# Spacing the expert and key/value matmuls between the key tiles of a four-layer attention kernel

## Chip, cores and metric

The kernel runs on one NeuronCore of one Trainium2 chip. The metric is the device time of one execution in microseconds (us), given as the median of repeated runs.

## What is computed

Four layers run one after the other on 1024 tokens of width 128. Each is a cross attention with 16 heads of width 8 over 6404 context rows, followed by a mixture of 8 experts. In the third layer (layer 2) the attention weights are a sigmoid, in the others a softmax. Cut to what matters:

```
for l in 0..3:
    h = layernorm(x);  q = h @ Wq.T + bq;  k = ctx @ Wk.T + bk;  v = ctx @ Wv.T + bv
    s = q_h @ k_h.T / sqrt(8)                    # 16 heads, 1024 x 6404 each
    a = sigmoid(s) if l == 2 else softmax(s)
    x = x + concat_h(a_h @ v_h) @ Wo.T + bo
    z = layernorm(x);  w = top-2 routing weights of 8 experts
    x = x + sum_e w_e * expert_e(z)              # gated (silu) in layers 0, 1, 3; gelu in layer 2
                                                 # layer 1 does this twice, on a normalised state
```

The result is x after the fourth layer, 1024 x 128.

## The kernel before, in words

**Tiling.** The 1024 tokens are two blocks of 512 (`QB`). A **unit** u is layer u // 2 and block u % 2 (`unit`), so there are eight. A unit's attention takes four **phases**, one for each group of four heads, so there are 32 phases, 0 to 31. A phase walks over the 6404 keys in 51 **key tiles** of 128. For a key tile the program issues: two `score` steps (each two matmuls, L798, into a pair of PSUM banks), two `exp` steps (ScalarE, L967, one for each pair, 128x1024), and one `av` step for the tile before (four fp32 matmuls, L808, two records of the profile each). In this document a key tile is counted from its first `exp`; a phase begins with every 102nd execution of L967.

**Maxima.** A softmax phase needs each query's largest score beforehand. It is found during the phase before: 176 `max` matmuls (L829, 128 queries by 512 keys, into one of three PSUM banks called `side`), each read by one `red` step of VectorE (L1081, for 32 of them L1085), and 16 `dif` pairs (L820), which ScalarE turns into `above` (`relu`, L975). That makes three to four `max` in each key tile and a `dif` in about every third. In the phases 15 to 22 and in phase 31 there are (almost) none, since the next phase is of the sigmoid layer or does not exist. At the end of a phase (from key tile 48 on) the `max` steps of the phase after the next one begin; they need `fill` (GpSimd, L1295), the copy of that phase's queries.

**Everything else runs beside the attention.** `finish_steps(u - 1)` is what follows the attention of unit u - 1: output projection, layernorm, routing, the experts (`pass_steps`) and the next layer's queries (`qproj`). It is placed into the phases of unit u. `kv_steps(l + 1)` computes keys and values of the next layer, in 13 chunks of two TensorE steps, during the first block of layer l. An expert has six TensorE steps in the gated layers: four `up` (fp32 matmul 128x512, L906) and two `down` (L924); in layer 2 it has eight, four of each. ScalarE reads each `up` with `tanh` and `ac` (L1008, L1017) or with `gc` (L1026), in layer 2 with `upc` (L1032); GpSimd then multiplies (`gatea`, `gateb`, `gatec`: L1362, L1368, L1372, L1378; in layer 2 `hscale`, L1384). In units 3, 4 and 7 VectorE does a part of that.

**PSUM.** The banks are two pairs (`scores`), three single banks (`side`) and one for `av`. `up`, `kv` and `qproj` steps in most units take a *pair* in turn with `score` and `dif`, and use one bank of it (`in_pairs`); `down` takes a `side` bank, in turn with `max`, and keeps it from its first matmul until ScalarE (`yc`) or VectorE has read the sum (`last_use`):

```
    def in_pairs(what, key):
        if what == "up":
            return not by_dve(*key[:2])
        return what in ("score", "dif") or what == "kv" and key[0] < 3 or ...
```

**What sets the order.** No scheduler runs on the chip. `attention_steps` writes one list of steps; each engine executes its own steps in that order, and waits in front of a step for what the step needs. Time in this list is counted in quarters of a key tile (`Q = 4 * KT`). `placed` gives each step of `finish_steps` or `kv_steps` a slot: it adds the gaps that the lists hold, and moves each TensorE step to the next free slot at `at % 4 == 1`. There is one such slot in each key tile, so at most one of these TensorE steps stands in a key tile. With the small gaps of `pass_steps` (0 or 1 inside the experts) that means one in *every* key tile from the first expert to the last. The steps of the other engines and the DMA issues take the slot of the TensorE step that they follow.

Of the kernel before, what the change touches and what calls it, by code (L numbers as in the profile page):

```python
# [118 lines left out]
def softmax(l):  # L119
    return l != 2  # L120


def unit(u):

    return u // 2, u % 2


def phase(p):

    return p // 8, p // NG % 2, p % NG  # L130
# [125 lines left out]
def kv_steps(l):  # L256

    out = []
    for c in range(NCH):
        out.append((1, Step("SP", "ctx", (l, c))))  # L260
        out.append((8, Step("PE", "kv", (l, c, 0))))
        out.append((0, Step("ACT", "kc", (l, c))))
        new = [n for n, (i, pair) in enumerate(SPLITS) if (2 * i + 1 if pair else i) == c]
        out += [(0, Step("POOL", "ksplit", (l, n))) for n in new]
        out.append((8, Step("PE", "kv", (l, c, 1))))
        out.append((0, Step("ACT", "vc", (l, c))))
        out += [(2, Step("SP", "kput", (l, n))) for n in new]
    return out


def norm_steps(u, tag):
    out = []
    if tag in ("f", "a"):
        out += [(2, Step("DVE", "sum", (u, tag))), (1, Step("DVE", "mean", (u, tag))), (1, Step("POOL", "center", (u, tag)))]
    out += [(1, Step("POOL", "square", (u, tag))), (7, Step("DVE", "sumsq", (u, tag))), (1, Step("POOL", "var", (u, tag))),
            (0, Step("POOL", "rstd", (u, tag))), (0, Step("POOL", "scale", (u, tag)))]
    if tag[0] == "r":
        out += [(1, Step("POOL", "weight", (u, tag)))]
    return out


def flip_steps(u, tag):
    return [(8, Step("PE", "xT", (u, tag))), (1, Step("ACT", "xTc", (u, tag)))]
# [82 lines left out]
def finish_steps(u):  # L366

    l, b = unit(u)
    out = []
    if u >= 0:  # L370
        if softmax(l):
            out += [(0, Step("POOL", "bvadd", (u,))), (0, Step("POOL", "boadd", (u,)))]
        out += [(8, Step("PE", "oflip", (u,))), (1, Step("ACT", "oflipc", (u,))), (4, Step("PE", "oproj", (u,))),
                (3, Step("DVE", "resid", (u,)))]
        out += norm_steps(u, "f")
        if l == 1:
            out.append((0, Step("POOL", "zcopy", (u,))))
        for lp in range(FFN[l]["loops"]):
            if l == 1:
                out += norm_steps(u, f"r{lp}")  # L380
            out += flip_steps(u, f"r{lp}" if l == 1 else "f")
            out += pass_steps(u, lp)
        if l == 1:
            out.append((1, Step("POOL", "zadd", (u,))))
    if l < 3:
        out += norm_steps(u, "a") + flip_steps(u, "a")
        for g in range(NG):
            out += [(1, Step("PE", "qproj", (u, g))), (0, Step("ACT", "qsplit", (u, g))), (0, Step("POOL", "qadd", (u, g)))]
    else:
        out.append((2, Step("SP", "out", (b,))))  # L390
    return out


def placed(at, steps, taken):


    out = []
    for gap, s in steps:
        at += gap
        if s is not None and s.eng == "PE":  # L400
            at += (1 - at) % 4
            while at in taken:
                at += 4
            taken.add(at)
        if s is not None:
            out.append((at, s))
    return out


def loads(u):  # L410

    l, b = unit(u)
    out = []
    if b:
        if l + 2 < 4:
            out += [(2, Step("SP", "wattn", (l + 2,))), (0, Step("DVE", "bqs", (l + 2,)))]
        if l + 1 < 4:
            out.append((0, Step("SP", "wo", (l + 1,))))
        out.append((0, Step("SP", "wffn", (l,))))
        if l == 3:  # L420
            out.append((0, Step("DVE", "b1s", (l,))))
    return out
# [3 lines left out]
            routee=1.0, routef=0.5, routeg=0.5, routeh=0.5, routej=0.5, routek=0.5, routel=0.5, routec=1.0, routed=0.4, gatea=0.7, gateb=0.7,  # L426
            ysum=0.7, upc=0.7)
Q = 4 * KT

LEAD = 12  # L430


def attention_steps(units):

    first, last = NG * units[0], NG * units[-1] + NG - 1
    back = []
    taken = set()
    for p in range(first, last + 1):
        at = p * Q
        if p + 1 < 32 and softmax(phase(p + 1)[0]):  # L440
            back += [(at + Q - LEAD - 1, Step("DVE", "fina", (p + 1,))), (at + Q - LEAD - 1, Step("DVE", "finb", (p + 1,))),
                     (at + Q - 7, Step("PE", "flipmax", (p + 1,))), (at + Q - 5, Step("DVE", "finc", (p + 1,)))]
            taken.add(at + Q - 7)
        if p > first:
# [5 lines left out]
        if p + 2 < 32:  # L450
            back.append((at + Q - LEAD - 4 if softmax(phase(p + 2)[0]) else at + 2 * Q - 8, Step("POOL", "fill", (p + 2,))))
            back += [(at + 4 * e + 2, Step("SP", "kload", (p + 2, i))) for i, (a, e) in enumerate(K_PIECES)]
            back += [(at + 6, Step("SP", "kload", (p + 2, len(K_PIECES) + i))) for i in range(NDIF)]
    for u in units:
        at = NG * u * Q
        if u:
            back += placed(at + 16, finish_steps(u - 1), taken)
    for u in units:
        l, b = unit(u)
        at = NG * u * Q  # L460
        back += placed(at + 2, loads(u), taken)
        if b == 0 and l < 3:
            back += placed(at + 24, kv_steps(l + 1), taken)
    back.sort(key=lambda x: x[0])

    def window(p):
# [151 lines left out]
def build(nc, A, out):  # L618
    ctx = ExitStack()
    with ctx:  # L620
# [1143 lines left out]
        with nc.If(n == P):  # L1764
            run(attention_steps(range(8)) + plain(finish_steps(7)))
        with nc.Else():
            layer0 = attention_steps([0, 1])
            masked_unit(0)
            run([s for s in layer0 if s.what not in in_attention + ("kv", "kc", "vc", "ksplit", "kput", "ctx")])
            masked_unit(1)  # L1770
            clear_values(1, 1)
            run([s for s in layer0 if s.what in ("kv", "kc", "vc", "ksplit", "kput", "ctx") or s.what in in_attention
                 and s.key[0] >= 8 and s.what not in ("score", "exp", "av")])
            run(attention_steps(range(2, 8)) + plain(finish_steps(7)))
# [74 lines left out]
```

## Time and profile before

| | |
|---|---|
| runs of the kernel | 4628.06, 4631.72, 4643.15 us; median 4631.72 us |
| the profiled execution, its own time | 4658.06 us |
| its span, first to last instruction | 4656.4 us |
| TensorE busy | 3974.0 us (85%) |
| ScalarE busy | 3939.7 us (85%) |
| VectorE busy | 2807.4 us (60%) |
| GpSimd busy | 830.0 us (18%) |
| granted TensorE clock, mean | 0.959 |

The profile is of one execution. Its span is the time between its first and last instruction; 1.7 us of its own time lie outside. "Busy" is the time in which at least one instruction of the engine runs. The 32 phases fill the span from 195.6 to 4564.7 us; before them lie the opening (first keys and values, first maxima), behind them the experts of unit 7.

### The profile page before, as it was taken

Reading aid. Unit: us, or ns where it says so; the run is one execution under the profiler, and the core shown is the slowest. Engines: PE = TensorE matmul, PEld = TensorE weight load, DVE = VectorE, ACT = ScalarE, POOL = GpSimd, SP = SyncE. Lnnn points to the kernel's source line nnn. Section 1 sums busy time; section 2 is a strip of 40 time slices with the busy share of each in tenths; the row PEclk is TensorE's granted clock in tenths of the full one; section 3 lists DMA queues with packets and bytes.
Section 4 is the critical chain, followed back from the end, with each engine's and each line's share of the span. In section 5 each row is a group of like instructions: output and inputs, shape, how many; then the busy total and the mean of one; then the engine's idle time right before and its main releaser. Section 6 shows DMA issues by size and latency. Waiting matters only on the chain.

```text
span 4656.4 us, 69652 instructions
## 1 busy us (share of the span) xinstructions
PE 3974.0 (85%) x26742; PEld 904.9 (19%) x26742; DVE 2807.4 (60%) x5641; ACT 3939.7 (85%) x4355; POOL 830.0 (18%) x719
## 2 busy tenths in 40 slices
PE   5988888888889888888989999888888888889886
PEld 2121111111122211122212222111111111112112
DVE  2878888778886788867501110110486668877823
ACT  3488998899988898888898889978998889888994
POOL 4010000520034200343412111111000210034002
PEclk8599999999999999999999999999999989999998
DMA  4221001100021110111102121110001100010001
GB/s 125 64 61 35 13 13 29 32 17 14 12 56 36 44 25 18 32 33 35 33 18 73 43 64 31 37 38 16 14 14 36 36 10 12 14 38 27 7 1 49
DMA packets 124485, 151.34 MB, mean 33 GB/s; under 512 B 29272, under 2 KB 76384, under 8 KB 124080
## 3 DMA queue, kind: packets, MB, share of 16 engines
q1 hardware_dynamic: 122640, 145.53, 11.7%
q8 instruction: 212, 3.47, 0.3%
q10 hardware_dynamic: 1504, 1.28, 0.2%
q14 instruction: 129, 1.06, 0.1%
HBM read 123.21 MB, written 23.51 MB: 32 GB/s over the span
## 4 chain that ended last, share of the span: by engine, by line
PE 50%; ACT 23%; DVE 15%; issue 6%; DMA 1%; POOL 0%; SPq 0%; ACTq 0%; POOLq 0%; DVEq 0%
PE av L808 19%; ACT prob L967 14%; DVE mpart L1081 10%; PE scores L798 10%; PE side L829 6%; ACT above L975 6%; PE scores L906 4%; DVE above L1085 4%; PE side L924 4%; PE side L906 2%; ACT ag L1017 1%; PE scores L820 1%; ACT tx L1008 1%; PE scores L948 1%; PE scores L944 1%
## 5 line engine op out<-in xcount | busy, mean ns | idle before, releaser
L967 ACT ACTIVATE prob<-scores 128x1024 f32<-128x1024 f32 x3264 | 3177.9, 1025 | 308.7 <-PE scores L798 293.7
L1081 DVE TENSOR_REDUCE mpart<-side 128x1 f32<-128x512 f32 (+1 forms) x3456 | 2124.3, 656 | 728.9 <-PE side L829 718.0
L808 PE MATMUL av<-prob,VA 128*9 128x512 f32 x6528 | 882.0, 613 | 0.8
L808 PE MATMUL av<-prob,VB 128*9 128x512 f32 x6528 | 867.4, 604 | 1.3 <-ACT prob L967 0.5
L798 PE MATMUL scores<-QP,KA 32*128 32x512 f16 x3264 | 640.1, 394 | 191.7 <-ACT above L975 120.4
L798 PE MATMUL scores<-QP,KB 32*128 32x512 f16 x3264 | 631.6, 389 | 191.4 <-ACT above L975 93.8
L829 PE MATMUL side<-KA,QP 32*128 32x512 f16 (+1 forms) x2112 | 624.7, 392 | 41.5 <-DVE mpart L1081 21.5
L829 PE MATMUL side<-KB,QP 32*128 32x512 f16 (+1 forms) x2112 | 583.0, 383 | 44.6 <-DVE mpart L1081 30.3
L1085 DVE CUSTOM_DVE_ANT_0 above<-side,above 128x512 f32<-128x512 f32 x768 | 513.8, 685 | 76.0 <-PE side L829 69.0
L975 ACT ACTIVATE above<-scores 128x1024 f32<-128x1024 f32 x384 | 393.5, 1025 | 180.9 <-PE scores L820 120.0
L798 PEld LDWEIGHTS scores<-QP,KB 32*128 32x128 f16 x3264 | 151.7, 91 | 865.9 <-ACT prob L967 535.3
L798 PEld LDWEIGHTS scores<-QP,KA 32*128 32x128 f16 x3264 | 151.4, 91 | 820.1 <-ACT prob L967 443.5
L829 PEld LDWEIGHTS side<-KA,QP 32*128 32x128 f16 x2112 | 147.4, 91 | 602.4 <-DVE mpart L1081 450.7
L829 PEld LDWEIGHTS side<-KB,QP 32*128 32x128 f16 x2112 | 140.5, 91 | 590.4 <-DVE mpart L1081 447.3
L906 PE MATMUL scores<-xnT,Fin 128*128 128x512 f32 (+1 forms) x256 | 147.0, 657 | 44.7 <-ACT above L975 31.0
L924 PE MATMUL side<-hT,Fout 128*128 128x512 f32 (+1 forms) x304 | 172.4, 654 | 8.5 <-POOL hT L1384 4.2
L1301 POOL TENSOR_TENSOR o_tok<-o_tok,bvo 128x512 f32<-128x512 f32 x6 | 7.7, 1278 | 898.9 <-DVE o_tok L1122 898.9
L1362 POOL TENSOR_TENSOR ag<-ag 128x512 f32<-128x512 f32 (+1 forms) x80 | 101.6, 1270 | 325.9 <-ACT ag L1026 325.9
L808 PEld LDWEIGHTS av<-prob,VA 128*9 128x9 f32 x6528 | 97.1, 88 | 196.0 <-issue 190.2
L808 PEld LDWEIGHTS av<-prob,VB 128*9 128x9 f32 x6528 | 97.0, 88 | 190.9 <-issue 183.3
L1112 DVE RECIPROCAL rden<-side 128x16 f32<-128x16 f32 x24 | 6.0, 249 | 206.1 <-PE side L847 206.1
L1411 POOL CAST hi<-kb 128x512 f16<-128x512 f32 (+1 forms) x60 | 35.7, 596 | 524.8 <-ACT kb L1056 513.7
(185 smaller groups left out, 2528.9 us busy)
## 6 DMA issues: line engine op xcount, KB each, us to landing
cwb<-weights SPq DMA_DIRECT2D x80, 256.0 KB, 3.9
KA<-kstacks SPq DMA_DIRECT2D x384, 48.0 KB
KB<-kstacks SPq DMA_DIRECT2D x384, 48.0 KB
Fin<-in_Fin SPq DMA_DIRECT2D x64, 256.0 KB, 2.8
kstacks<-hi SPq DMA_DIRECT2D x112, 128.0 KB, 2.4
ctxc<-in_ctxT SPq DMA_DIRECT2D x36, 256.0 KB, 3.0
kstacks<-lo SPq DMA_DIRECT2D x56, 128.0 KB, 2.6
hT<-in_mask SPq DMA_DIRECT2D x16, 400.2 KB, 3.3
```

The lines of the kernel that those rows point to most:

```text
L798: last = pe.matmul(pair[:, j, :], K[p % 2][rows(h), kt * P:kt * P + P], QP[p % 3][rows(h), :], start=True, stop=True)
L808: last = pe.matmul(AV[ROWS * h:ROWS * h + VC, :], V[l % 2][:, kt, g * HG + h, :], prob[:, (e + h // 2) % RING, (h % 2) * QB:(h % 2) * QB + ...
L820: last = pe.matmul(pair[:, j, :], QP[p % 3][rows(h), qt * P:(qt + 1) * P], K[p % 2][rows(h), difference(i)], start=True, stop=True)
L829: pe.matmul(bank[:, 0:chunk_of(c)], QP[p % 3][rows(h), qt * P:(qt + 1) * P], K[p % 2][rows(h), chunk(c)], start=True, stop=True).then_inc( ...
L906: pe.matmul(bank[0:fs, :], Fin[:, w, j * fs:(j + 1) * fs], x[:], start=True, stop=True).then_inc(sem["bgP"], 1)
L924: pe.matmul(bank, Fout[0:fs, w, c, :], h, start=first, stop=c == nk - 1).then_inc(sem["bgP"], 1)
L944: last = pe.matmul(bank[:, 0:w], Wk[l % 2][:], context(l, c)[:, 0:w], start=True, stop=True)
L967: act.activation(prob[:, e % RING, :], pair.rearrange("p a b -> p (a b)"), ACT.Exp if softmax(l) else ACT.Sigmoid, scale=SCALE).then_inc(s ...
L975: act.activation(above[:].rearrange("p a b -> p (a b)"), pair.rearrange("p a b -> p (a b)"), ACT.Relu).then_inc(sem["bgA"], 1)
L1081: dve.tensor_reduce(part, bank, AX.X, ALU.max).then_inc(sem["red"], 1)
L1085: dve.tensor_tensor_reduce(more, bank, more, 1.0, LEAST, ALU.add, ALU.max, part).then_inc(sem["red"], 1)
L1362: pool.tensor_tensor(a, a, g, ALU.mult).then_inc(sem["bgG"], 1)
```

## The change

`placed` gets a parameter `pace`, counted in key tiles. A TensorE step is not placed earlier than `pace` key tiles after the place that the step before it was due (`beat`). With 1.0, the value before, nothing changes. The experts behind the units 0, 1, 2, 5 and 6 get 2.0, 1.7, 1.3, 1.7 and 2.8; the keys and values of layers 1 and 2 get 4.0 and 5.0. Those behind the units 3 and 4 and the keys and values of layer 3, which run where there are no maxima, stay as they are. Six lines are added to the file, so line numbers behind them are larger by 6 afterwards.

```
-def placed(at, steps, taken):
+def placed(at, steps, taken, pace=1.0):
     out = []
+    beat = at
     for gap, s in steps:
         at += gap
         if s is not None and s.eng == "PE":
+            at = max(at, int(beat))
             at += (1 - at) % 4
             while at in taken:
                 at += 4
             taken.add(at)
+            beat = max(beat, at - 4 * pace) + 4 * pace
         if s is not None:
             out.append((at, s))
     return out
...
+PACE = {0: 2.0, 1: 1.7, 2: 1.3, 5: 1.7, 6: 2.8}
+KV_PACE = {1: 4.0, 2: 5.0}
...
         if u:
-            back += placed(at + 16, finish_steps(u - 1), taken)
+            back += placed(at + 16, finish_steps(u - 1), taken, PACE.get(u - 1, 1.0))
...
         if b == 0 and l < 3:
-            back += placed(at + 24, kv_steps(l + 1), taken)
+            back += placed(at + 24, kv_steps(l + 1), taken, KV_PACE.get(l + 1, 1.0))
```

What it does to the number of these TensorE steps (of `finish_steps` and `kv_steps`) in each phase, counted in the list that each version writes:

| phases | before | now |
|---|---|---|
| 0, 1, 2, 3 | 17, 9, 0, 0 | 12, 12, 2, 0 |
| 4, 5, 6, 7 | 25, 35, 0, 0 | 17, 26, 17, 0 |
| 8, 9, 10, 11 | 33, 42, 11, 0 | 28, 40, 18, 0 |
| 12, 13, 14, 15 | 23, 34, 46, 8 | 20, 35, 31, 25 |
| 16 to 23 | 32, 41, 49, 15, 27, 43, 5, 0 | the same |
| 24, 25, 26, 27 | 26, 44, 5, 0 | 19, 30, 26, 0 |
| 28, 29, 30, 31 | 26, 28, 0, 0 | 14, 18, 19, 3 |

How it looks on TensorE in phase 29 (experts of unit 6), key tiles 9 and 10. Before (L798 are the scores, L829 the maxima, L808 the `av` step, L906 an expert's `up`):

```order
L798 MATMUL scores<-QP,KB 128x512 x2
L829 MATMUL side<-KA,QP 128x512
L906 MATMUL scores<-xnT,Fin 128x512
L798 MATMUL scores<-QP,KB 128x512 x2
L829 MATMUL side<-KA,QP 128x512 x2
L808 MATMUL av<-prob,VB 9x512 x4
L829 MATMUL side<-KA,QP 128x260
L798 MATMUL scores<-QP,KB 128x512 x2
L829 MATMUL side<-KA,QP 128x260
L906 MATMUL scores<-xnT,Fin 128x512
L798 MATMUL scores<-QP,KB 128x512 x2
```

The same two key tiles now (L804, L835, L814 and L912 are the same four):

```order
L804 MATMUL scores<-QP,KB 128x512 x2
L835 MATMUL side<-KA,QP 128x260
L912 MATMUL scores<-xnT,Fin 128x512
L804 MATMUL scores<-QP,KB 128x512 x2
L835 MATMUL side<-KA,QP 128x260
L835 MATMUL side<-KA,QP 128x512
L814 MATMUL av<-prob,VB 9x512 x4
L835 MATMUL side<-KA,QP 128x512
L804 MATMUL scores<-QP,KB 128x512 x2
L835 MATMUL side<-KA,QP 128x512
L804 MATMUL scores<-QP,KB 128x512 x2
```

Before, each key tile has one `up`; now one of the two has one, and the next comes later still.

TensorE in phase 6, key tiles 4 and 5, which belonged to the attention alone. Before:

```order
L829 MATMUL side<-KB,QP 128x512 x2
L808 MATMUL av<-prob,VA 9x512 x4
L798 MATMUL scores<-QP,KA 128x512 x2
L829 MATMUL side<-KB,QP 128x512
L798 MATMUL scores<-QP,KA 128x512 x2
L829 MATMUL side<-KB,QP 128x512 x2
L808 MATMUL av<-prob,VA 9x512 x4
L829 MATMUL side<-KB,QP 128x512
L820 MATMUL scores<-KB,QP 128x512 x2
```

Now (L930 is `down` of an expert of unit 0, L826 a `dif` pair):

```order
L804 MATMUL scores<-QP,KA 128x512 x2
L930 MATMUL side<-hT,Fout 128x512
L804 MATMUL scores<-QP,KA 128x512 x2
L835 MATMUL side<-KB,QP 128x512 x2
L814 MATMUL av<-prob,VA 9x512 x4
L835 MATMUL side<-KB,QP 128x512
L804 MATMUL scores<-QP,KA 128x512 x2
L835 MATMUL side<-KB,QP 128x512
L930 MATMUL side<-hT,Fout 128x512
L804 MATMUL scores<-QP,KA 128x512 x2
L835 MATMUL side<-KB,QP 128x512 x2
```

Expert steps now stand between the maxima of a phase that had none.

GpSimd at the end of phase 28, before (L1362 to L1378 are the four products of a chunk of an expert, L1393 adds an expert's result, L1295 is the `fill`):

```order
L1393 TENSOR_TENSOR sq<-sq,yb 128x512
L1362 TENSOR_TENSOR ag<-ag 128x512
L1368 TENSOR_SCALAR tx<-tx 128x512
L1372 TENSOR_TENSOR hT<-tx,ag 128x512
L1378 TENSOR_TENSOR hT<-hT,cwb 128x512
L1295 COPY QP<-Qst 128x512
L1362 TENSOR_TENSOR ag<-ag 128x512
```

And now:

```order
L1378 TENSOR_TENSOR hT<-tx,ag 128x512
L1384 TENSOR_TENSOR hT<-hT,cwb 128x512
L1301 COPY QP<-Qst 128x512
L1396 COPY sq<-yb 128x512
L1368 TENSOR_TENSOR ag<-ag 128x512
```

The `fill` still stands right behind a chunk's four products; what is now further away is the chunk before that one.

## Rows read from the trace of the kernel before

**Rows 1.** The page: busy time by engine, and the chain that ended last.

```profile
PE 3974.0 (85%) x26742; PEld 904.9 (19%) x26742; DVE 2807.4 (60%) x5641; ACT 3939.7 (85%) x4355; POOL 830.0 (18%) x719
...
PE 50%; ACT 23%; DVE 15%; issue 6%; DMA 1%; POOL 0%; SPq 0%; ACTq 0%; POOLq 0%; DVEq 0%
```

**Rows 2.** Phases 4, 5, 6, 18, 31: length; PE, PEld, DVE, ACT, POOL busy; clock.

```profile
732.00:881.60 149.60, 128.41 (x899) 28.95 (x899) 115.49 (x256) 129.37 (x150) 43.45 (x36) 0.97 0.12 34
881.60:1032.60 151.00, 132.85 (x900) 29.62 (x900) 111.50 (x216) 135.12 (x160) 57.42 (x47) 1.00 0.08 22
1032.60:1155.70 123.10, 100.63 (x828) 20.07 (x828) 107.73 (x214) 112.41 (x121) 0.61 (x1) 1.00 0.05 13
...
2683.90:2818.90 135.00, 134.80 (x720) 31.05 (x719) 27.17 (x40) 113.72 (x123) 13.26 (x13) 1.00 0.20 56
...
4468.90:4564.70 95.80, 86.03 (x614) 15.97 (x614) 0.55 (x2) 95.53 (x104) 0.00 (x0) 1.00 0.00 1
```

**Rows 3.** ScalarE's order of time in phase 6: start, us, what [idle before].

```profile
1096.04 1.02 ACT L975 ACTIVATE above<-scores 128x1024 f32<-128x1024 f32 x1 [0.56 <-PE scores L820]
1096.96 3.86 ACT L967 ACTIVATE prob<-scores 128x1024 f32<-128x1024 f32 x4
```

**Rows 4.** Waits in phase 6, key tiles 4 to 27: who, on whom, us, times, longest.

```profile
PEld side L829 <- DVE mpart L1081: 14.5, 19, 0.9
...
PEld side L829 <- DVE mpart L1085: 7.3, 11, 0.9
```

**Rows 5.** Stretches: packed (phase 5) and quiet, kv (phase 1) and quiet.

```profile
893.60:971.00 77.40, 69.93 (x444) 15.09 (x444) 55.30 (x107) 68.75 (x84) 40.44 (x31) 1.00 0.08 23
1044.00:1102.40 58.40, 47.24 (x393) 8.94 (x393) 53.30 (x108) 53.94 (x57) 0.00 (x0) 1.00 0.05 11
364.70:413.60 48.90, 41.96 (x333) 11.47 (x333) 39.48 (x82) 44.75 (x52) 6.93 (x9) 1.00 0.20 51
1044.00:1086.50 42.50, 35.15 (x293) 6.62 (x293) 38.99 (x81) 39.73 (x43) 0.00 (x0) 1.00 0.04 10
```

**Rows 6.** Stretches: packed, then quiet, of phases 29, 13 and 25.

```profile
4205.00:4288.50 83.50, 74.19 (x460) 17.13 (x459) 57.00 (x111) 74.03 (x89) 47.34 (x37) 1.00 0.11 31
1036.60:1097.00 60.40, 49.27 (x412) 9.58 (x408) 54.57 (x110) 55.88 (x61) 0.00 (x0) 1.00 0.05 13
1997.00:2092.60 95.60, 85.00 (x518) 18.98 (x516) 65.46 (x126) 80.10 (x97) 45.45 (x35) 0.98 0.10 29
1036.60:1104.40 67.80, 54.96 (x460) 10.63 (x456) 60.62 (x122) 62.57 (x68) 0.00 (x0) 1.00 0.05 11
...
3622.50:3673.90 51.40, 48.60 (x293) 11.42 (x293) 35.90 (x70) 41.48 (x48) 5.71 (x3) 0.96 0.10 29
1042.10:1079.40 37.30, 31.05 (x259) 5.88 (x259) 33.88 (x69) 35.06 (x39) 0.00 (x0) 1.00 0.05 12
```

**Rows 7.** ScalarE's order of time in phase 1, ahead of and behind a `kc`.

```profile
378.62 1.02 ACT L967 ACTIVATE prob<-scores 128x1024 f32<-128x1024 f32 x1
...
380.53 3.93 ACT L967 ACTIVATE prob<-scores 128x1024 f32<-128x1024 f32 x4
```

**Rows 8.** Waits before the `up` matmuls (L906) of unit 5, by what ended them.

```profile
  DMA Fout<-in_Fout: 5.0, 3
```

**Rows 9.** Order of time on all engines at the end of phase 28.

```profile
4187.79 1.26 POOL L1378 TENSOR_TENSOR hT<-hT,cwb 128x512 f32<-128x512 f32 x1
4189.00 0.61 POOL L1295 COPY QP<-Qst 128x512 f16<-128x512 f16 x1
4189.67 0.10 PEld L829 LDWEIGHTS side<-KA,QP 32*128 32x128 f16 x1 [2.70 <-issue]
...
4190.32 0.69 DVE L1081 TENSOR_REDUCE mpart<-side 128x1 f32<-128x512 f32 x1 [9.13 <-PE side L829]
```

**Rows 10.** The stretch behind that stall.

```profile
4189.70:4196.20 6.50, 6.50 (x24) 1.59 (x25) 2.95 (x5) 2.53 (x4) 2.89 (x3) 0.50 0.00 0
```

**Rows 11.** GpSimd's `hscale` of layer 2, by group: count, busy, mean ns.

```profile
L1384 POOL TENSOR_TENSOR hT<-hT,cwb 128x1024 f32<-128x1024 f32 x12 | 27.9, 2349 | 177.4 <-ACT hT L1037 177.4
```

More of the change, by code:

```diff
@@ L391, in finish_steps, with placed @@
     return out
-def placed(at, steps, taken):
+def placed(at, steps, taken, pace=1.0):
     out = []
+    beat = at
     for gap, s in steps:
@@ L400, in placed @@
         if s is not None and s.eng == "PE":
+            at = max(at, int(beat))
             at += (1 - at) % 4
@@ L404, in placed @@
             taken.add(at)
+            beat = max(beat, at - 4 * pace) + 4 * pace
         if s is not None:
@@ L428 @@
 Q = 4 * KT
+PACE = {0: 2.0, 1: 1.7, 2: 1.3, 5: 1.7, 6: 2.8}
+KV_PACE = {1: 4.0, 2: 5.0}
 LEAD = 12
@@ L456, in attention_steps @@
         if u:
-            back += placed(at + 16, finish_steps(u - 1), taken)
+            back += placed(at + 16, finish_steps(u - 1), taken, PACE.get(u - 1, 1.0))
     for u in units:
@@ L462, in attention_steps @@
         if b == 0 and l < 3:
-            back += placed(at + 24, kv_steps(l + 1), taken)
+            back += placed(at + 24, kv_steps(l + 1), taken, KV_PACE.get(l + 1, 1.0))
     back.sort(key=lambda x: x[0])
```

## The prediction

> **What bounds the kernel now.** First the page: TensorE and ScalarE are each busy for 85% of the span, and the chain that ended last runs half over TensorE, then ScalarE and VectorE [rows 1]. No engine is full, and no single one is the chain, so the share over the whole span decides nothing. The second view is the busy time by stretch, with one stretch for each phase. Phase 6, which has the attention and the maxima and nothing else, takes 123.1 us; phase 5, with 35 expert steps, takes 151.0 [rows 2]. A quiet phase is not free of idle time either: TensorE is busy for 100.6 us of its 123.1, ScalarE for 112.4, VectorE for 107.7. The question is whether steps that move from phase 5 into phase 6 find room in that idle time.
>
> The third view is the order of time on ScalarE in phase 6. Four `exp` in a row take 3.86 us, so about 0.95 us from start to start; but before the `relu` of each `dif`, in every third key tile or so, ScalarE waits 0.56 us for TensorE [rows 3]. The fourth view, the waits, says why: in 24 key tiles of this phase TensorE's maxima wait 14.5 + 7.3 = 21.8 us for VectorE to hand back a `side` bank [rows 4]. So where nothing else runs the cycle of three key tiles (58.40 / 24 x 3 = 7.3 us [rows 5]) is partly VectorE's, and it leaves ScalarE some 0.6 us.
>
> **The price of a packed step.** I compare stretches with the same key tiles of a quiet phase.
> - Unit 0, phase 5, key tiles 4 to 27: 77.40 against 58.40 us with 24 steps [rows 5], 19.0 / 24 = **0.79 us** each.
> - Unit 6, phase 29, key tiles 1 to 25: 83.50 against 60.40 with 24 steps [rows 6], **0.96**.
> - Unit 2, phase 13, key tiles 1 to 28: 95.60 against 67.80 with 27 steps, **1.03**.
> - Unit 5, phase 25, key tiles 3 to 18: 51.40 against 37.30 with 16 steps, **0.88**.
>
> **The price of a spaced step.** The trace has no spaced experts. The nearest rows are the key/value steps, one in every second key tile: phase 1, key tiles 4 to 21, has eight, and takes 48.90 us where the quiet phase takes 42.50 [rows 5], so 6.4 / 8 = **0.80**. They take a pair like `up` and one read by ScalarE. The bounds: at most nothing is hidden. In a key tile without a `dif`, the two `exp` around a `kc` start at 378.62 and 380.53, 1.91 us apart in place of 0.95 [rows 7], so 0.96, call it 1.0. At least, the first step of each three-tile cycle hides in the 0.6 us of rows 3 and the others cost 1.0; at a pace of 2, with 1.5 steps in a cycle, (1.5 - 0.6) / 1.5 = 0.6. I take 0.80, since it is measured at nearly the density that the change makes, and keep 0.6 and 1.0.
>
> **The change, part by part.** It adds no instruction that computes; it moves steps.
> - *Unit 6 (pace 2.8).* All 48 expert steps become spaced: 48 x (0.96 - 0.80) = **-7.7 us**. Its end moves from phase 29 into phase 31 (three steps there), and nobody waits for it, as unit 7's experts come after the last phase.
> - *Unit 5 (1.7).* 64 expert steps: 64 x (0.88 - 0.80) = **-5.1**. Its weights arrive late three times, 5.0 us of wait [rows 8]; the load of expert k + 3 is issued behind `down` of expert k, and with 1.7 times as long until its use that wait should go: **-5.0**. The stalls behind the double gelu remain, as many as before. Its last `qproj` now stands in key tile 46 of phase 26, one tile ahead of the `fill` that needs the first of them; it fits.
> - *Unit 2 (1.3).* Three tenths of the way from packed to spaced: 0.07 on the 35 + 31 steps of phases 13 and 14, **-4.6**. 17 steps go to phase 15, which has no maxima. There a step costs as in phase 18, (135.0 - 95.8) / 49 = 0.80 [rows 2], so 17 x (1.03 - 0.80) = **-3.9**.
> - *Units 0 and 1, keys and values.* Unit 0 goes from 0.79 to 0.80: 0. Unit 1 and layer 2's keys and values together hardly change their density (33, 42, 11 to 28, 40, 18): 0. Layer 1's keys and values were spaced already: 0.
> - *The `fill` at the end of phase 28.* Before, GpSimd is behind with two chunks, `fill` starts at 4189.00 and TensorE stands still for 2.7 us at its first `max` [rows 9]; behind it the clock is at its lower level, 1.2 GHz (granted 0.50), for 6.5 us [rows 10]. So 2.7 us are lost at once, and up to half of the 6.5 again: some 5. Now one chunk stands ahead of `fill` with nothing late behind it. A chunk is four products like the one of 1.26 us [rows 9], a little over 5 us, against the 7 us that three key tiles take. But in phase 25 the four `hscale` of 2.35 us [rows 11] now stand four key tiles ahead of a `fill`, 9.4 us against some 10: a new, smaller stall may come there. Together **-2**.
>
> SP's queue keeps its order of loads with the steps they follow, and GpSimd has 82% of the span free, so I cost both at nothing; where that cover fails is in the last item.
>
> The sum is -7.7 - 5.1 - 5.0 - 4.6 - 3.9 - 2 = **-28 us**. The profiled execution would go from 4658 to 4630. It lies 26 us above the median of the runs shown, which I take as the base: 4632 - 28 = **4604 us**, 0.6% less.
>
> A rule on the clock speaks against thinner TensorE work. The trace first: in phase 6 TensorE has only 101 us of work in 123 and the granted clock is 1.00 [rows 2]; it fell where TensorE stood still and then waited on one bank [rows 9, 10]. The Trainium skill, "TensorE: Matmul & The Clock Gate", in "Why this matters for your kernels", says that matmuls should come densely, as an idle gap sends the clock back to half. By the trace a spaced phase is dense enough, so this adds nothing to the sum unless a step's wait makes such a gap.
>
> **The rivals.**
>
> *A: the two kinds of phase fill each other's gaps.* Quiet phases lose time to VectorE, packed ones to TensorE and ScalarE; once every cycle has one step, each hides the full 0.6 us. A spaced step then costs 0.6: unit 0 saves 48 x 0.19 = 9, unit 6 48 x 0.36 = 17, unit 5 64 x 0.28 = 18, unit 2 about 14, and 7 for the two waits: -65, 4567 us. For it: the 21.8 us of waits on VectorE [rows 4]. Against it: the eight spaced steps of phase 1 did not hide like that. The Trainium skill, "Perfetto Trace Analysis", in "Optimization Strategy", says that a kernel whose most-contended engine changes over time may gain from interleaving its regimes; it would speak for this case.
>
> *B: the price does not depend on the spacing.* In phase 5 and phase 1 it is 0.79 and 0.80. The 0.96 and 1.03 of units 6 and 2 may come from their four GpSimd products and longer reads, not from packing; then only the waits change, -7 at the best, and 0 if new ones come: about 4628 us.
>
> *C, slower: `down` keeps a `side` bank.* Its first matmul takes one of the three banks and gives it back only when `yc` has read the second. Packed, that is one key tile; at a pace of 2.8 it is almost three, and in unit 5, where four `down` alternate with `up`, nearly all the time. Meanwhile the maxima have two banks. Before, where VectorE has slack, this hardly shows. In the phases that are new to experts TensorE already waits 21.8 / 24 = 0.9 us in each key tile for a bank [rows 4]; if a third fewer banks make that wait half as long again, it is 0.45 us for each held tile, and about 100 key tiles are held in addition (16 for unit 0, 22 more for unit 6, some 40 for unit 5, the rest for units 1 and 2): +45. Net of the gains +17, so 4649 us. It decides from 28 / 100 = 0.28 us for each held tile. Against it: a `max` and its `red` take about 1.1 us in sum, so two banks would still feed VectorE every 0.55 us.
>
> That the change does not do what it says can be left out: the order of TensorE's instructions shows it.
>
> **How the numbers follow.** Forecast 0.45, A 0.18, B 0.22, C 0.15. A measurement of this kernel tells about 0.3%, 14 us, from no change. Faster by more than that: A and most of the forecast, 0.18 + 0.40 = 0.58. Within 0.3%: B, the forecast's weak end, some of C, 0.20 + 0.05 + 0.02 = 0.27. Slower: 0.15. The range reaches from A's 4567 to C's near side, 4644; outside lie a stronger A and most of C, together near 0.2. With 0.6 and 1.0 in the forecast's own sum it would be 4567 to 4637.
>
> **What would show it.** In the profile after: phases 4 to 6 together near 424 us (before 149.6 + 151.0 + 123.1 = 423.7), phases 28 to 31 10 to 14 us shorter than before, 24 to 26 about 10, 12 to 15 about 8; phase 28's last key tiles at a granted clock of 1.00; the `up` matmuls of unit 5 without a wait on DMA. Rival A is right if phases 4 to 6 fall by 9 or more; B if the price by step in unit 6 stays at 0.96; C if the waits of L829's successor on VectorE, or on `yc`, grow in phases 6, 26 and 30 by more than the time saved. The forecast is wrong if `fill` comes late in phases 25, 28 or 29, which would show as idle TensorE at key tile 48 and a clock of 0.50 behind it.

## The result, and the profile after

The changed kernel is slower: 4660.39 us (median of 4 runs, 4656.02 to 4661.93) against 4634.73 us (median of 4 runs of the kernel before), a ratio of 1.0053 with a 95% interval of 1.0034 to 1.0072. A second comparison beside the experiments gave 1.0039 (1.0023 to 1.0054). The forecast was 28 us less, with 15 in 100 for slower, and 4660 lies outside its range.

Single executions of one and the same kernel differ here by up to 35 us, so the totals of two profiles say little: the two profiled executions have spans of 4656.4 and 4659.4 us. Phases can be compared, since most phases that the change doesn't touch come back within 0.1 us, except where the clock falls. A fall from 1.00 to 0.99 in a phase goes with about 1.2 us (phase 3 of the kernel before: 123.7 and 124.9 us). Phase 20 is a larger case. Its instructions are the same in both kernels; it takes 133.9 us in the profile after and 128.1 us in a later execution of the kernel before, and its granted clock is 0.91 and 0.96. In the first profile of the kernel before it took 134.0 us, so this difference is not the change's. Each line has the stretch in us from the span's start, its length, the busy time (and number) of TensorE's matmuls, its weight loads, VectorE, ScalarE and GpSimd, the granted clock, and the DMA engines' busy share and GB/s. First of the changed kernel:

```profile
2919.70:3053.60 133.90, 120.31 (x689) 26.39 (x689) 17.02 (x47) 110.23 (x114) 14.15 (x10) 0.91 0.13 37
```

and of a second profile of the kernel before (`before_again` below):

```profile
2912.30:3040.40 128.10, 114.17 (x689) 25.94 (x689) 17.00 (x47) 110.28 (x114) 14.16 (x10) 0.96 0.13 39
```

The phases that changed, in the changed kernel (4, 5, 6; then 8, 9, 10; then 28, 29, 30):

```profile
720.70:859.30 138.60, 116.27 (x881) 26.66 (x881) 113.97 (x254) 122.77 (x139) 27.76 (x24) 1.00 0.12 32
859.30:1006.90 147.60, 126.85 (x882) 27.77 (x882) 111.28 (x216) 131.03 (x153) 47.73 (x37) 1.00 0.09 26
1006.90:1143.90 137.00, 118.23 (x864) 25.84 (x864) 110.13 (x216) 123.37 (x139) 25.89 (x23) 0.99 0.05 11
1268.70:1415.30 146.60, 128.46 (x925) 32.95 (x925) 115.18 (x247) 129.18 (x150) 47.88 (x44) 1.00 0.19 51
1415.30:1575.80 160.50, 140.77 (x940) 34.35 (x940) 112.18 (x216) 140.28 (x167) 60.61 (x50) 1.00 0.16 45
1575.80:1717.90 142.10, 118.32 (x888) 28.31 (x888) 110.16 (x216) 124.28 (x140) 21.27 (x22) 0.99 0.10 25
4038.70:4180.90 142.20, 117.28 (x875) 27.14 (x875) 112.02 (x244) 121.46 (x136) 28.49 (x24) 0.98 0.09 25
4180.90:4331.30 150.40, 126.42 (x865) 26.98 (x863) 108.93 (x214) 125.75 (x140) 35.30 (x28) 0.95 0.09 24
4331.30:4470.80 139.50, 119.46 (x855) 26.01 (x855) 103.78 (x203) 125.41 (x141) 36.42 (x28) 1.00 0.04 11
```

The phases 4 to 6 take 423.2 us, as before (423.7 [rows 2]): what phase 4 and 5 lose, phase 6 gains. The phases 8 to 10 and 28 to 30 are longer than in the second profile of the kernel before:

```profile
1274.70:1424.80 150.10, 131.97 (x937) 33.73 (x937) 115.93 (x250) 133.15 (x157) 56.59 (x50) 1.00 0.20 54
1424.80:1582.50 157.70, 139.80 (x935) 33.65 (x935) 111.95 (x216) 139.94 (x166) 63.14 (x54) 1.00 0.12 33
1582.50:1715.00 132.50, 110.41 (x884) 27.26 (x881) 108.30 (x214) 119.41 (x131) 10.02 (x13) 1.00 0.15 37
4027.10:4181.20 154.10, 131.09 (x901) 30.79 (x901) 114.20 (x246) 131.17 (x150) 51.46 (x42) 0.98 0.11 32
4181.20:4326.40 145.20, 130.05 (x883) 28.86 (x882) 109.18 (x213) 130.69 (x150) 50.32 (x39) 0.99 0.10 26
4326.40:4448.50 122.10, 99.58 (x815) 19.65 (x815) 102.03 (x204) 111.37 (x119) 0.00 (x0) 1.00 0.01 2
```

That is 449.2 against 440.3 us (+8.9) and 432.1 against 421.4 (+10.7). TensorE's busy time hardly moves (363.2 in place of 360.7 in the last three); it is the time around it that grows. With phases 11 and 31 the two groups are 10.2 and 12.0 us longer. Phases 4 to 7 are 1.2 us longer than in the same profile, 12 to 15 and 24 to 27 are 1.5 and 3.0 us shorter: +18.9 us in all five. Phases 16 to 23, which the change leaves alone, are 12 us longer at a lower clock, and phase 0 is 9 us shorter at a higher one (0.91 and 0.87); these two are not put down to the change.

One cause stands at the end of phase 29, in the order of time (start, us, engine and line, [idle before]; L1384 is the last of a chunk's four products, L1301 the `fill`, L835 a `max`, L973 an `exp`):

```profile
4313.84 1.26 POOL L1384 TENSOR_TENSOR hT<-hT,cwb 128x512 f32<-128x512 f32 x1
4315.05 0.61 POOL L1301 COPY QP<-Qst 128x512 f16<-128x512 f16 x1
...
4315.76 0.58 PE L835 MATMUL side<-KB,QP 32*128 32x512 f16 x1 [1.67 <-issue]
...
4318.93 1.02 ACT L973 ACTIVATE prob<-scores 128x1024 f32<-128x1024 f32 x1 [3.77 <-PE scores L804]
```

It is the stall of [rows 9], now in phase 29 too: the `fill` (L1301) comes out of GpSimd behind a chunk's products, the first `max` (L835) waits for it, and ScalarE then sits idle for 3.77 us. Key tiles 48 and 49 of phase 29 take 8.1 and 5.3 us, where before they took 2.8 and 2.2; the stall of phase 28 is still there too (7.8 us for key tile 48, 8.6 before). Behind the 1.67 us in which TensorE stood still the clock is at its lower level, 1.2 GHz, for 17.1 us, although TensorE is busy for 15.2 of them:

```profile
4315.40:4332.50 17.10, 15.21 (x57) 2.97 (x57) 7.87 (x13) 6.95 (x7) 0.26 (x1) 0.50 0.00 0
```

The price of a step alone, which I had no row for, can now be read in phase 30, key tiles 4 to 26:

```profile
4343.60:4407.50 63.90, 54.00 (x393) 11.43 (x393) 50.82 (x101) 58.54 (x67) 17.09 (x13) 1.00 0.04 11
```

The same 23 key tiles of a quiet phase in the kernel before:

```profile
1044.00:1098.90 54.90, 44.95 (x375) 8.52 (x375) 49.80 (x101) 51.14 (x55) 0.00 (x0) 1.00 0.05 12
```

There are nine expert steps in the first and none in the second: 9.0 / 9 = **1.0 us** for each, the upper bound of the prediction, and as much as they add to TensorE's busy time (54.00 - 44.95). The stretch is dearer than its phase, though. The whole of phase 30 gives (139.5 - 122.2) / 19 = **0.91 us**, phase 6 (137.0 - 123.1) / 17 = 0.82, and both include what the banks kept by `down` cost.

### The profile page after: what moved, and what is told of

Read it like the earlier page. It is cut to its first block, busy times and chain, and to the rows that moved or that the text cites. A ratio compares the mean times of both kernels' runs of the same rounds, so it can differ in the third digit from the quotient of the medians.

```text
span 4659.4 us, 69643 instructions
## 1 busy us (share of the span) xinstructions
PE 3971.5 (85%) x26742; PEld 908.0 (19%) x26742; DVE 2808.3 (60%) x5641; ACT 3940.1 (85%) x4355; POOL 829.9 (18%) x719
## 4 chain that ended last, share of the span: by engine, by line
PE 50%; ACT 24%; DVE 14%; issue 6%; DMA 1%; SPq 1%; POOL 0%; POOLq 0%; ACTq 0%; DVEq 0%
PE av L814 19%; ACT prob L973 14%; PE scores L804 10%; DVE mpart L1087 9%; PE side L835 7%; ACT above L981 6%; PE scores L912 4%; DVE above L1091 4%; PE side L930 4%; PE side L912 2%; PE scores L826 1%; ACT ag L1023 1%; ACT tx L1014 1%; PE scores L954 1%; PE scores L950 1%
## 5 line engine op out<-in xcount | busy, mean ns | idle before, releaser
L973 ACT ACTIVATE prob<-scores 128x1024 f32<-128x1024 f32 x3264 | 3181.2, 1025 | 323.9 <-PE scores L804 309.5
L814 PE MATMUL av<-prob,VA 128*9 128x512 f32 x6528 | 875.7, 609 | 1.0
L814 PE MATMUL av<-prob,VB 128*9 128x512 f32 x6528 | 864.1, 602 | 1.1 <-ACT prob L973 0.5
L804 PE MATMUL scores<-QP,KA 32*128 32x512 f16 x3264 | 638.6, 391 | 193.3 <-ACT above L981 111.4
L804 PE MATMUL scores<-QP,KB 32*128 32x512 f16 x3264 | 631.4, 389 | 190.6 <-ACT above L981 102.5
L835 PE MATMUL side<-KA,QP 32*128 32x512 f16 (+1 forms) x2112 | 624.3, 392 | 50.0 <-DVE mpart L1087 26.8
L835 PE MATMUL side<-KB,QP 32*128 32x512 f16 (+1 forms) x2112 | 582.8, 380 | 50.3 <-DVE mpart L1087 33.6
L804 PEld LDWEIGHTS scores<-QP,KB 32*128 32x128 f16 x3264 | 152.2, 91 | 856.5 <-ACT prob L973 498.9
L804 PEld LDWEIGHTS scores<-QP,KA 32*128 32x128 f16 x3264 | 151.9, 91 | 819.1 <-ACT prob L973 451.2
L835 PEld LDWEIGHTS side<-KA,QP 32*128 32x128 f16 x2112 | 147.6, 91 | 612.8 <-DVE mpart L1087 453.8
L835 PEld LDWEIGHTS side<-KB,QP 32*128 32x128 f16 x2112 | 143.0, 91 | 597.6 <-DVE mpart L1087 456.1
L912 PE MATMUL scores<-xnT,Fin 128*128 128x512 f32 (+1 forms) x256 | 146.9, 656 | 43.7 <-ACT above L981 34.9
L930 PE MATMUL side<-hT,Fout 128*128 128x512 f32 (+1 forms) x304 | 174.1, 659 | 8.8 <-POOL hT L1390 4.2
L814 PEld LDWEIGHTS av<-prob,VA 128*9 128x9 f32 x6528 | 97.0, 88 | 192.0 <-issue 185.3
L1399 POOL TENSOR_TENSOR sq<-sq,yb 128x512 f32<-128x512 f32 x42 | 53.3, 1270 | 452.3 <-ACT yb L1048 452.3
L814 PEld LDWEIGHTS av<-prob,VB 128*9 128x9 f32 x6528 | 96.9, 88 | 189.4 <-issue 182.0
```

The lines of the kernel that those rows point to most:

```text
L804: last = pe.matmul(pair[:, j, :], K[p % 2][rows(h), kt * P:kt * P + P], QP[p % 3][rows(h), :], start=True, stop=True)
L814: last = pe.matmul(AV[ROWS * h:ROWS * h + VC, :], V[l % 2][:, kt, g * HG + h, :], prob[:, (e + h // 2) % RING, (h % 2) * QB:(h % 2) * QB + ...
L835: pe.matmul(bank[:, 0:chunk_of(c)], QP[p % 3][rows(h), qt * P:(qt + 1) * P], K[p % 2][rows(h), chunk(c)], start=True, stop=True).then_inc( ...
L912: pe.matmul(bank[0:fs, :], Fin[:, w, j * fs:(j + 1) * fs], x[:], start=True, stop=True).then_inc(sem["bgP"], 1)
L930: pe.matmul(bank, Fout[0:fs, w, c, :], h, start=first, stop=c == nk - 1).then_inc(sem["bgP"], 1)
L973: act.activation(prob[:, e % RING, :], pair.rearrange("p a b -> p (a b)"), ACT.Exp if softmax(l) else ACT.Sigmoid, scale=SCALE).then_inc(s ...
```

## The experiments

Twelve runs were made: both kernels again, and ten edited ones. The executions' spread of 35 us would hide most effects in the totals, so I read the phases, each from one profiled execution. Where two lists are the same in a unit's phases, its sum still came back up to 3.5 us apart (phases 12 to 15: 566.7 to 570.2 us, with the clock). Differences of 1 to 3 us below are no more than hints.

**1. Both kernels again.** No edit.

> The kernel before once more, for a profile taken beside the others. The two profiled executions shown so far differ by 3 us only (4658.1 and 4661.1), the medians by 26 (4634.7 and 4660.4). Theory 1: the profiled execution of the kernel before was one of its long ones, and a new one has a span near 4635, with the 20 us missing in one or a few places that the two profiles of this kernel show side by side. Theory 2: profiling changes the time of the kernel before by 20 us each time, then the span is again near 4656.

> The changed kernel once more, beside the others. Theory 1 expects a ratio of 1.005 to the kernel before and the same time in each phase as in its first profile, within 0.3 us. If the 20 us depend on the execution rather than on the kernel, this one should show a time near 4640 at least once.

Measured: the kernel before 4637.97 us (span of the profiled execution 4636.6), the changed one 4658.27 us, ratio 1.0039 (1.0023 to 1.0054), span 4675.0. Theory 1 holds for the first: 12 us of the 20 lie in phases that are the same instructions in both kernels, where the clock fell more or less (phases 16 to 23: 1032.5 us in the first profile, 1020.2 in the second). For the changed kernel "within 0.3 us" failed in eleven phases, by 1.2 to 5.5 us (5.5 in phase 0, 5.0 in 26, 4.4 in 29). No execution of the changed kernel came near 4640 us (lowest 4650.72), so the loss belongs to the kernel.

**2. The copy of the queries earlier**, in both kernels, by 24 quarters of a key tile, that is six key tiles:

```
-            back.append((at + Q - LEAD - 4 if softmax(...) else ...
+            early = 24 if (p + 2) % NG >= 2 else 0
+            back.append((at + Q - LEAD - 4 - early if softmax(...) else ...
```

> The changed kernel with the copy of the queries (fill) six key tiles earlier in the phases whose expert work can delay it. Theory: the stalls at the ends of phases 28 (key tile 48: 7.8 us in place of about 2.9) and 29 (key tiles 48 and 49: 8.1 and 5.3 in place of 2.8 and 2.2) are GpSimd's lateness with the fill, so both go: -5 and -8, with the half clock behind them, 4660 to about 4646. Rival: these tiles are long since down holds a side bank there; then the early fill changes nothing, within 1 us.

> The kernel before with the same early fill. Theory: only the stall at key tile 48 of phase 28 (8.6 us in place of 3.9) goes, -5 us, the other phases stay within 0.3 us. Rival: nothing changes.

Measured: 4650.05 us, ratio 1.0019 (1.0003 to 1.0035), and 4633.46 us, ratio 0.9987 (0.9966 to 1.0008). Phases 28 to 31 fall from 529.1 to 520.9 us in the changed kernel (535.0 in its second profile) and from 517.2 to 514.7 in the kernel before. The stalls go, as the first theory said: phase 29 has 144.0 us and a clock of 0.99 in place of 150.4 and 0.95:

```profile
4030.70:4170.00 139.30, 117.87 (x875) 26.98 (x875) 112.18 (x243) 121.34 (x135) 28.53 (x24) 0.98 0.09 26
4170.00:4314.00 144.00, 121.53 (x865) 26.48 (x863) 108.93 (x214) 125.67 (x141) 35.30 (x28) 0.99 0.09 25
4314.00:4454.60 140.60, 120.42 (x855) 25.86 (x855) 103.78 (x203) 125.48 (x140) 36.38 (x28) 0.99 0.04 11
```

So about 6 of the 12 us that phases 28 to 31 lost (8.2 less the 2.5 that the kernel before gains too) are the late `fill`. Both gains are smaller than expected (13 and 5 us). In the other phases nothing of the loss goes: phases 4 to 7 take 549.7 us in place of 548.0, and 8 to 11 573.6 in place of 575.3.

**3. The `down` steps of an expert side by side**, in the changed kernel with the early fill:

```
-            at = max(at, int(beat))
+            if s.what != "down" or s.key[-1] == 0:
+                at = max(at, int(beat))
```

> The changed kernel with the early fill, and with the later down steps of an expert free of the pace: they take the next slot behind the first, so a side bank is held as briefly as before. Rival C of the prediction (the held bank) expects the phases 4 to 6, 8 to 10 and 28 to 30 to become shorter by some 4 us each, together over 10 us of the 20 that the changed kernel lost. Theory L (a step alone in a cycle of three key tiles costs 1.0 us wherever it stands, a packed one about 0.8) expects a part of this, as two downs side by side are cheaper than two alone: about 0.2 to 0.3 us for each of the 24 experts, 5 to 7 us in all.

Measured: 4645.49 us, ratio 1.0016 (0.9997 to 1.0034). By units against `after_fill_early`: phases 4 to 7 -1.8, 8 to 11 -1.9, 12 to 15 -2.8, 28 to 31 -8.0 us (520.9 to 512.9). Together -14.5, in the direction of rival C and more than theory L gives, but not 4 us in each: over half is in unit 6, whose pace is the longest. The phases 24 to 27 (unit 5) go the other way, from 596.1 to 599.9 us, nearly all in phase 25, at a clock of 0.92 in place of 0.95; so the five units together give -10.7. The phases 28 to 30 as one stretch, of `after_fill_early`:

```profile
4030.70:4454.60 423.90, 359.82 (x2592) 79.31 (x2592) 324.89 (x659) 372.50 (x415) 100.22 (x80) 0.98 0.07 20
```

of `downs_together`:

```profile
4035.00:4450.60 415.60, 353.88 (x2592) 78.97 (x2592) 324.70 (x659) 373.08 (x415) 100.37 (x80) 1.00 0.08 21
```

and of `before_fill_early`:

```profile
4019.30:4438.10 418.80, 360.81 (x2598) 79.49 (x2598) 325.42 (x660) 373.11 (x416) 101.69 (x81) 0.99 0.08 21
```

Part of the 8 us is thus the clock, 1.00 in place of 0.98. With the bank given back at once the spaced experts of unit 6 take 3.2 us less than the packed ones in these three phases, where with both faults they took 10.7 more. Three of their steps stand in phase 31; with it 1.8 us are left, which the spread of executions can make.

**4. The held bank by itself.** The kernel before with the early fill and a distance of two key tiles, once between the downs (the held bank, below) and once ahead of them (the twin, which has `== 0` in place of `== 1`), in units 0, 1 and 6:

```
         if s is not None and s.eng == "PE":
+            if s.what == "down" and s.key[0] in (0, 1, 6) and s.key[-1] == 1:
+                at += 8
```

> The kernel before with the early fill, and in the units 0, 1 and 6 two key tiles of distance between the two downs of an expert; everything else is packed as before. The side bank is held for two key tiles more, 48 in all. To be read against its twin, down_shifted, which has the same distance ahead of the first down. Theory C (the held bank): 0.15 to 0.4 us for each held tile, so phases 4 to 6, 8 to 10 and 28 to 30 are each 2 to 6 us longer than in the twin. Theory L (only the number of steps alone in a cycle counts): the same up to 2 us, since the downs alone are dearer than side by side by 0.3 us at most.

> The twin: the same two key tiles of distance, but ahead of the first down of an expert, so that no bank is held in them. If spacing as such costs nothing, phases 4 to 6 together equal those of the kernel before with the early fill (423.4 us), 28 to 30 too (418.8 us), within 1 us; if a part of the loss is the spacing, they are 1 to 4 us longer.

Measured, phases 28 to 30, 4 to 6 and 8 to 10, with the bank held (in these two kernels L832 is a `max` and L1084 its `red`):

```profile
4056.80:4482.90 426.10, 363.34 (x2598) 79.83 (x2598) 327.37 (x660) 373.04 (x416) 101.78 (x81) 0.99 0.08 21
730.30:1161.50 431.20, 365.39 (x2627) 79.79 (x2627) 336.41 (x684) 377.93 (x427) 101.36 (x84) 1.00 0.09 23
1287.50:1737.70 450.20, 391.36 (x2753) 95.75 (x2753) 337.52 (x678) 393.55 (x453) 129.61 (x116) 0.99 0.15 41
```

and in the twin:

```profile
4033.90:4455.20 421.30, 358.55 (x2598) 79.11 (x2598) 325.74 (x660) 373.20 (x417) 101.74 (x81) 0.99 0.08 21
721.30:1149.60 428.30, 364.35 (x2627) 79.61 (x2627) 335.14 (x684) 376.88 (x428) 101.39 (x84) 0.99 0.09 23
1274.40:1722.30 447.90, 388.28 (x2753) 95.33 (x2753) 337.17 (x678) 392.37 (x454) 129.53 (x116) 0.99 0.15 41
```

The held bank costs 4.8, 2.9 and 2.3 us, 10.0 for 48 held key tiles: **0.21 us each**. Each unit rests on one execution of each kernel; all three have the sign and the size (2 to 6 us) that theory C expected. It shows in the waits of the maxima's weight loads on VectorE in phases 28 to 30 (us, times, longest), held:

```profile
PEld side L832 <- DVE mpart L1084: 120.3, 159, 2.7
```

and in the twin:

```profile
PEld side L832 <- DVE mpart L1084: 103.7, 138, 2.5
```

The twin also shows a cost without a held bank: against `before_fill_early` (418.8, 423.5 and 441.5 us) its stretches are 2.5, 4.8 and 6.4 us longer, 13.7 in all. "Spacing costs nothing", within 1 us, is refuted, though in phases 8 to 10 the clock was also lower in the twin (0.99 against 1.00). The whole executions took 4671.75 and 4644.52 us, one run each, which I don't use.

**5. Which steps cost in phases 8 to 11.** The changed kernel with the early fill and other paces:

```
-PACE = {0: 2.0, 1: 1.7, 2: 1.3, 5: 1.7, 6: 2.8}
-KV_PACE = {1: 4.0, 2: 5.0}
+PACE = {0: 1.4, 6: 1.7}
+KV_PACE = {2: 5.0}
```

> The changed kernel with the early fill and other paces: unit 0 at 1.4, unit 6 at 1.7, units 1, 2 and 5 at 1.0, keys and values of layer 2 still at 5.0, those of layer 1 without. Theory L: phases 12 to 15 and 24 to 26 equal those of the kernel before; phases 4 to 6 within 2 us of both; phases 28 to 30 between before and changed, +2 to +4 us. Phases 8 to 10 tell where their +8 us come from: if from the spaced keys and values they stay at +6 or more, if from unit 1's experts they fall back to under +3.

Measured, sums of the unit's phases against `before_fill_early` (`after_fill_early` in brackets): 8 to 11 566.4 and 566.3 us (573.6), 28 to 31 514.1 and 514.7 (520.9), 4 to 7 553.1 and 548.2 (549.7), 24 to 27 599.7 and 597.2, 12 to 15 570.2 and 566.7. So the 7 us of phases 8 to 11 come with the spacing of unit 1's experts, not with that of the keys and values. Unit 6 at 1.7 costs nothing, where +2 to +4 was expected. Unit 0 at 1.4 costs 5 us where 2.0 costs 1.5, which I didn't expect: the price doesn't follow the pace in one line. The units 2 and 5 are spaced as in the kernel before, so their +3.5 and +2.5 us are the spread of executions. The whole execution took 4660.49 us (one run).

**6. VectorE with half of the work.** Both kernels with the early fill; the maxima are taken over half of each chunk's keys only:

```
-dve.tensor_reduce(part, bank, AX.X, ALU.max)
+dve.tensor_reduce(part, bank[:, 0:chunk_of(c) // 2], AX.X, ALU.max)
```

(and the same for the pairs that read `above`).

> The kernel before with the early fill; each of VectorE's reads of the maxima covers half of its columns (the maxima are taken over half of the keys). If VectorE sets the pace of a quiet phase, phases 2, 6, 11, 27 fall from 123 to 125 us to about 113, ScalarE's share in them (102 exp and 16 relu at 0.92 to 0.95 us). If they fall by less than 3 us, they are bound by the handing over between TensorE and ScalarE. The packed phases 5 and 9 should hardly change (under 4 us).

> The changed kernel with the early fill and the same halved reads. If the spaced steps are dear because VectorE starves while TensorE does them, the difference to the unspaced twin in phases 28 to 30, and 8 to 10, changes sign or goes to zero here. If it is the pair of banks and ScalarE's order, the difference stays at +5 to +8 us for each of the two units.

Measured: phases 6 and 27 of `light_before`:

```profile
964.90:1082.60 117.70, 99.54 (x828) 20.40 (x828) 65.87 (x214) 112.31 (x120) 0.61 (x1) 1.00 0.06 14
3768.20:3887.30 119.10, 100.09 (x831) 20.58 (x831) 66.99 (x217) 113.29 (x121) 0.00 (x0) 1.00 0.06 14
```

VectorE's busy time falls from 107.7 us [rows 2] to 65.9, the phase only from 123.1 to 117.7. That is between the 10 us of "VectorE sets the pace" and the under 3 of "it does not". ScalarE's idle time in the phase, 123.1 - 112.4 = 10.7 us, shrinks to 5.4: half of it goes with VectorE's work, and the other half stays. That this half is the handing over between TensorE and ScalarE is argued, not shown. The packed phases 5 and 9 fell by nearly as much (4.3 and 4.2 us), so VectorE's part in the time is much the same in both kinds of phase. Between the two kernels phases 28 to 30 differ by 3.5 us here:

```profile
3887.30:4288.20 400.90, 349.45 (x2598) 78.05 (x2598) 201.10 (x659) 372.55 (x417) 101.60 (x81) 1.00 0.08 22
```

before, and changed:

```profile
3899.80:4304.20 404.40, 350.66 (x2592) 77.74 (x2592) 201.77 (x658) 371.96 (x415) 100.31 (x80) 1.00 0.08 21
```

where with full reads it is 5.1 (418.8 and 423.9), and in phases 8 to 11 3.7 in place of 7.3. A quick VectorE takes away at most a part of the loss and doesn't turn it into a gain: between the two theories. The whole executions took 4475.9 and 4492.79 us, one run each.

**7. Denser instead.** Two slots in each key tile, in the kernel before with the early fill (`at += (1 - at) % 2`, and `at += 2` where a slot is taken).

> The other way: the kernel before with the early fill and two slots in each key tile for these steps in place of one, so that experts are packed twice as densely. Theory L has no gain left (a packed step costs 0.75 to 0.96 in any case) and expects GpSimd's four products for each chunk, 5.3 us, against two chunks in three key tiles, to become what TensorE waits for in the units 0, 1, 2 and 6: +5 to +30 us. If the price keeps falling with density, -10 us.

Measured: 4753.59 us (one run), +114 on the kernel before; more than the 30 us at most that I had expected. The loss is in every unit, in the phases 12 to 15 alone 596.3 us in place of 566.7, and in 16 to 27 another 43. Phases 28 and 29 take 180.4 and 123.6 us, 304.0 in place of 295.4. Key tiles 28 to 50 of phase 28, with 45 expert steps:

```profile
4214.50:4317.50 103.00, 95.22 (x465) 23.63 (x466) 52.22 (x94) 82.60 (x108) 88.07 (x69) 1.00 0.15 42
```

The same key tiles of phase 6 take 53.3 us (1102.4 to 1155.7), so a step costs 49.7 / 45 = 1.1 us there; stretches with one step in a key tile gave 0.96 [rows 6], those with spaced steps 1.0. GpSimd is not what TensorE waits for, as I had expected: in this stretch it waits for GpSimd once, for 0.9 us, and is itself busy for 92% of the time. Why the other units lose more I haven't followed.

**8. A choice of units.** Early fill, downs together, paces for the units 2, 5 and 6 alone:

```
+PACE = {2: 1.3, 5: 1.7, 6: 2.8}
+KV_PACE = {}
```

> The early fill, downs together, and the pace only for the units 2 (1.3), 5 (1.7) and 6 (2.8), without one for keys and values and for the units 0 and 1. By the phases of the runs so far: 28 to 31 as in downs_together (512.9 us, -2 against before_fill_early), 12 to 15 -2, 24 to 27 -1 to +2, all else as before_fill_early. So 4 to 5 us less than before_fill_early, about 0.2% below the kernel before; within the spread of its executions that may not be told from it.

Measured: 4636.04 us, ratio 0.9989 (0.9977 to 1.0001). Its phases sum to 3.3 us less than those of `before_fill_early`, where 4 to 5 was expected. But these lie in phases 0 to 7, which are the same in both lists (4.3 us less, with the clock). The units that were chosen bring nothing: phases 12 to 15 -0.4, 24 to 27 +1.3, 28 to 31 -0.6. The interval just reaches 1, and the kernel is not told apart from the kernel before or from the early fill alone.

## Why the prediction was wrong

**The price of a packed step** failed first, for unit 6. I took 0.96 us from 25 key tiles of phase 29 [rows 6]. The phase as a whole says (144.4 - 123.1) / 28 = 0.76: its other half, from 4288.5 to 4346.7, has four more steps in 58.2 us, and the same key tiles of the quiet phase take 58.7 (1097.0 to 1155.7). A stretch cut out of a phase left its cheaper part behind. With 0.76 the term of -7.7 us has no base. Unit 2's 1.03 has the same fault: the whole of phase 13 gives (152.6 - 123.1) / 34 = 0.87.

**The price of a spaced step**, "I take 0.80", failed next: in unit 6 it is 0.91 over the whole of phase 30, and 1.0 in a stretch of it. The eight steps of phase 1 [rows 5] stood one in every second key tile, and the experts at a pace of 2.8 one in three. More room between steps did not make them cheaper but dearer, 0.91 in place of 0.76 by whole phases. For 48 steps that is +7 us where -7.7 was forecast; with the early fill in both kernels phases 28 to 31 measure +6.2. With the downs side by side the whole of phase 30 gives (137.3 - 122.2) / 18 = 0.84, so a part of the 0.91 is the held bank. Rival A is refuted: a spaced step costs 0.82 to 0.91 and not 0.6, and with half of VectorE's work taken away a quiet phase gets only 5.4 us shorter. Rival B, the same price at any spacing, comes nearer but has no place for 0.76 against 0.91.

**Unit by unit.** Units 0 and 5: 0 and -5.1 forecast; 4 to 7 went by 0 to +3 us, 24 to 27 by 0 to -3 in total where -10 was forecast. The wait of unit 5's `up` matmuls for their weights did go (5.1 us, three times, in the second profile of the kernel before; none in the changed one), so that term had its cause right, and what it gave was used up by dearer steps. Unit 2's -8.5 came out as some -1 us, within what the clock changes: 15 steps left phase 14 for -17.7 us, 17 came to phase 15 for +17.2, so that a step there costs 1.0 and not the 0.80 of phase 18. Unit 1 was costed at 0 since its density hardly changes; it costs 7 us, as `pace_sweep` shows.

**The fill** was the right mechanism with the wrong sign. I saw the stall and its half clock, and that a chunk ahead of the `fill` is 5 us; I took three key tiles of 7 us as enough cover, and looked for new trouble in phase 25. It came in phase 29, and phase 28's stall stayed: together +6 us in place of -2. The stall's price, 5 us, was about right for key tile 48 of phase 28 (8.6 us, and 3.9 with the early fill), but over phases 28 to 31 the kernel before gained only 2.5 from its going.

**Rival C** was right in its mechanism and too high in its price and its count: 0.21 us for each held key tile, where I had 0.45, and 52 more held key tiles by the two lists (6, 5 and 1 in the units 0, 1 and 2, 27 in unit 5, 13 in unit 6), where I had about 100. That would be 11 us in place of 45, if the price held in unit 5 too, which is not shown: there the downs side by side made it longer. In the other four units `downs_together` holds a bank for 23 key tiles less than the changed kernel, some 5 us at this price; the rest of its 14.5 us is the clock and whatever two downs side by side save, which I have not told apart. The rival was to decide "from 0.28 us for each held tile" against 28 us of gains; there were no such gains, so a smaller price is enough for a loss.

**The sum**, then: where the forecast had -28, the early fill takes back some 6 us and the downs side by side 10.7. What stays is 4 us: 5.4 in phases 8 to 11 and 2.7 in 24 to 27, less 4.2 in the other three units. The medians go the same way: 4660, 4650, 4645 against 4635 to 4640; the intervals of neighbouring ratios overlap, so each step by itself rests on the phases.

**What stays open.** Why spacing without a held bank costs 2.5 to 6.4 us in a unit (`down_shifted`), why unit 1 loses 7 us, and why unit 0 is dearer at 1.4 than at 2.0. It may matter which of the steps fall on a key tile with a `dif`; no run here tries an order that sees to it.

## What to carry to other kernels

When idle time is spread through a pipeline of engines that hand over a few banks, do not count it as a reserve: here a step that went in cost three quarters or more of the 1.0 us that it adds on TensorE, packed or spaced. Measure such a price over whole phases, not over a stretch cut out of them. Before a step is stretched out, look at what it holds while it waits (a PSUM bank here) and who else takes turns for it. And put small copies that start the next phase well ahead of large work in the same queue.

## What the runs showed of the hardware

An unchanged stretch took 128.1 or 133.9 us (phase 20), at a granted clock of 0.96 or 0.91. The phases 16 to 23, the same instructions in both kernels, differ by 12 us between two executions of the kernel before; what decides whether the clock falls there I did not find out. Behind the 2.7 us in which TensorE stood still its clock was at the lower of its two levels, 1.2 GHz, for at least 6.5 us [rows 9, 10]; key tile 48 of that phase took 8.6 us and 3.9 without the pause, so the pause cost nearly as much again as it lasted. The length of the pause does not give the length of the slow stretch: behind 1.67 us in phase 29 of the changed kernel it was 17.1 us, with TensorE busy for 15.2 of them. A PSUM bank held for a key tile more, of the three that the maxima go through, cost 0.21 us.
